# First pass in place: transposed rows written over x, sixteen tiles kept on chip, el and er twelve tiles behind, four statistics groups

## The chip, the cores and the metric

One core of one Trainium2 chip runs the kernel. The metric is device time in microseconds (us) of one execution. The engines are TensorE (PE, and PEld for its weight loads), VectorE (DVE), ScalarE (ACT), GpSimd (POOL) and SyncE (SP, which only issues transfers). SBUF is the on-chip memory of 128 partitions, PSUM the banks that TensorE writes.

## What is computed

Two layers of a graph network over N = 6250 nodes, E = 100000 edges sorted by dst, D = 512 features and 8 heads. In short form:

```python
h  = relu(layernorm(x))                                  # first pass
el = einsum((h @ W_src + b_src), attn_l)                 # per node and head
er = einsum((h @ W_dst + b_dst), attn_r)
v  = h @ W_val + b_val
e  = leaky_relu(el[src] + er[dst], 0.2)
a  = softmax of e over the edges of one dst
x  = x + segment_sum(v[src] * a, dst)                    # attention neighbour stage
h  = relu(layernorm(x))
x  = x + two GCN layers(h): relu(D^-1/2 (A + 2I) D^-1/2 h W + b), each
```

## The kernel before

The 6250 nodes are 49 tiles (TILES) of 128 rows. The order of the work is written by hand: every engine has its own program, and semaphores join them. What one engine waits for holds everything behind it in its program, its transfers included.

**First pass.** x is loaded in chunks of 8 tiles (XL) into `big`: three chunks from ScalarE's queue, three and the last tile from SP's, behind the weights. VectorE takes the statistics of each tile (`statistics`), and makes scale and bias for a group of tiles (`moments`), with a square root on ScalarE between (`deviations`). The groups are GROUPED = (0, 8, 24, 49). ScalarE normalises tile k into a buffer in `rows`; TensorE transposes it into a bank `tr`; ScalarE copies the bank to one of four buffers `ht_out` (HT = 4); TensorE multiplies that copy with 16 columns of folded weights into `sm` (this gives el and er, one tile behind the transposes); SP stores the copy to `ht_tab` in HBM. A buffer is free again when its store has landed and its product is done: `act.wait_ge(ht_kept[t % HT], t // HT * 16)` (L1340). Every fourth tile ScalarE copies el and er of four tiles (L1348) and TensorE turns them back (L1556). The folded weights come from GpSimd products (L1206, L1207) that wait for both pairs of weights, and from VectorE reductions (L492, L494).

**The row search.** VectorE compares node numbers with borders of the dst list (`find_rows`, L510), GpSimd then fetches rows of the list by indirect transfers (`seek_ring`, L1216), seven to a group, and VectorE counts in them (`count_in_rows`, L523). It ends in the in-degree of every node and its place in the edge list.

**V tiles.** v = h W_val is made tile by tile from the transposed rows. ScalarE reloads them from `ht_tab` into `ht_ring` (L1317), TensorE makes a tile with 4 matmuls of 512 columns (`value`, L1566), ScalarE copies it out (L1361) and stores it to `v_tab` (L1365). TensorE fills its waits with these tiles: V1 = 14 of them stand between the small products that prepare the tables (L1579 to L1607), ahead of the one-hot **picks** of el[src] (L1621, from 207 to 570 us); the other 35 stand among the edge softmax's waits. V_AT tells after how many tiles TensorE takes up each of the three carries of VectorE's scans (L1657, L1661); W_AT after how many it turns a half block of edge weights (L1650, eight of them, copied out alternately by VectorE at L834 and ScalarE at L1394); EXP_AT ahead of which tile ScalarE runs the two exponentials (L1385). VectorE clears `big` in two pieces at the end (L838, L841). Then GpSimd gathers rows of V, two gathers of 128 rows to a unit (L1280, 782 in all), once all V tiles are stored.

```python
V_AT = (V1 + 11, V1 + 19, V1 + 29)
EXP_AT = (V1 + 25, V1 + 25)
W_AT = (V1 + 32, V1 + 32, V1 + 33, V1 + 33, V1 + 34, V1 + 34, TILES, TILES)
```

Of the kernel before, what the change touches and what calls it, by code (L numbers as in the profile page):

```python
# [68 lines left out]
GROUPED = (0, 8, 24, TILES)  # L69
# [5 lines left out]
Q = 4  # L75
# [5 lines left out]
V1 = 14  # L81
V_AT = (V1 + 11, V1 + 19, V1 + 29)
EXP_AT = (V1 + 25, V1 + 25)
W_AT = (V1 + 32, V1 + 32, V1 + 33, V1 + 33, V1 + 34, V1 + 34, TILES, TILES)
HT = 4
ER_LOAD = 104
# [36 lines left out]
def build(nc, x, src, dst, W_src, b_src, W_dst, b_dst, W_val, b_val, attn_l, attn_r, W1, b1, W2, b2, out):  # L123
    ctx = ExitStack()
    with ctx:
# [140 lines left out]
        below = part(SEEK * (ROW // 2 + 1)).bitcast(BF16).rearrange("p (s n) -> p s n", s=SEEK)  # L266
# [23 lines left out]
        scanned = part.at  # L290
        ht_ring = part(HT * D).rearrange("p (s n) -> p s n", s=HT)
        ringed = part.at
# [11 lines left out]
        g_from = part(CUT.blocks ** 2 * P // 2).bitcast(BF16).rearrange("p (g n) -> p g n", n=CUT.blocks * P)  # L304

# [6 lines left out]
        def ht_out(slot):  # L312
            return rows[:, (4, 5, 0, 1)[slot], :]
# [4 lines left out]
        def first(t):  # L318
# [15 lines left out]
        pad_set, const_set, ident_set, edges_kept, fold_in, edges_in, dst_in = map(sem, (  # L334
            "pad_set", "const_set", "ident_set", "edges_kept", "fold_in", "edges_in", "dst_in"))
# [11 lines left out]
        wval_in, fold_loads = fold_in, 6  # L347
# [13 lines left out]
        ht_kept, low_before = low_in, [16 * len(range(n, TILES, HT)) for n in range(HT)]  # L361
# [41 lines left out]

        def all_kept(eng, pair, per=16):
            eng.wait_ge(pair[0], per * ((TILES + 1) // 2))
            eng.wait_ge(pair[1], per * (TILES // 2))
# [17 lines left out]

        prep, pe_steps = [0], [0]
# [3 lines left out]
        def _(dve):  # L429
# [38 lines left out]
            def moments(n, at):  # L468
# [9 lines left out]
                dve.scalar_tensor_tensor(ln[:, 1, at], ln[:, 3, at], 0.25, ln[:, 2, at], ALU.mult, ALU.add).then_inc(ln_set, 1)  # L478
                dve.wait_ge(std_set, n + 1)
# [6 lines left out]
            moments(0, slice(0, GROUPED[1]))  # L486
            statistics(range(1, 2))

            for s in range(2):
# [6 lines left out]
            dve.wait_ge(folded, 10)  # L496
            statistics(range(2, 3))
            dve.wait_ge(stat_set, GROUPED[2])
            moments(1, slice(GROUPED[1], GROUPED[2]))

# [51 lines left out]
            moments(2, slice(GROUPED[2], TILES))  # L552
# [17 lines left out]

            dve.wait_ge(h_set, TILES)
# [233 lines left out]
            dve.wait_ge(std_set, 4)  # L805
# [204 lines left out]
        def _(sp):  # L1010
# [4 lines left out]
            sp.dma_start(W_src_sb[:, :, :], W_src.rearrange("(k p) n -> p k n", p=P)).then_inc(fold_in, 16)  # L1015
            sp.dma_start(attn_sb[:, 0, :], on_all(attn_l.rearrange("h f -> (h f)"))).then_inc(fold_in, 16)
            sp.dma_start(bsd_sb[:, 0, :], on_all(b_src)).then_inc(fold_in, 16)
            sp.dma_start(W_dst_sb, W_dst.rearrange("(k p) n -> p k n", p=P)).then_inc(fold_in, 16)
            sp.dma_start(attn_sb[:, 1, :], on_all(attn_r.rearrange("h f -> (h f)"))).then_inc(fold_in, 16)
            sp.dma_start(bsd_sb[:, 1, :], on_all(b_dst)).then_inc(fold_in, 16)  # L1020
# [22 lines left out]
            for t in range(TILES):  # L1043
                sp.wait_ge(hT_set, t + 1)
                sp.dma_start(ht_tab[t, :, :], ht_out(t % HT)).then_inc(ht_kept[t % HT], 16)
                if t in (8, 11):
                    sp.wait_ge(edges_kept, 64)
                    load_firsts((8, 11).index(t))
                if t == 22:
                    sp.dma_start(src_flat[:, 0:J], src_rows.rearrange("g e -> (g e)").rearrange(  # L1050
                        "(p j) -> p j", j=J)).then_inc(edges_in, 16)
                if t == 26:
                    sp.dma_start(dst_i, dst_flat).then_inc(dst_in, 16)
                if t == 30:
                    sp.wait_ge(folded, 10)
                    sp.dma_start(wmat[:, :, 0:D], W_val.rearrange("(k p) n -> p k n", p=P)).then_inc(wval_in, 16)
                if t == 36:
# [8 lines left out]
            sp.wait_ge(h_set, TILES)  # L1066
            sp.wait_ge(dve_prep, marks["ends_of_units"])
# [6 lines left out]
            for n in range(HT):  # L1074
                sp.wait_ge(ht_kept[n], 16 * len(range(n, TILES, HT)))
# [105 lines left out]
        def _(pool):  # L1181
# [22 lines left out]
            pool.wait_ge(fold_in, 16 * fold_loads)  # L1204
            for s, w in enumerate((W_src_sb, W_dst_sb)):
                pool.tensor_tensor(bfold[:, s, :], bsd_sb[:, s, :], attn_sb[:, s, :], ALU.mult).then_inc(dve_setup, 1)  # L1206
                pool.tensor_tensor(fold[:, s, :, :], w[:, :, :], attn_sb[:, s, :].unsqueeze(1).to_broadcast([P, KC, D]),  # L1207
                                   ALU.mult).then_inc(dve_setup, 1)
            pool.wait_ge(edges_kept, 64)
            by_row = dst_rows.rearrange("g e -> (g e)").rearrange("(r e) -> r e", e=ROW)  # L1210
# [8 lines left out]
            pool.wait_ge(h_set, TILES)  # L1219
# [90 lines left out]
        def _(act):  # L1310
# [5 lines left out]
            def load_ht(t, slot):  # L1316
                act.dma_start(ht_ring[:, slot, :], ht_tab[ds(t, 1), :, :].rearrange("a p n -> p (a n)")).then_inc(ht_in[slot], 16)  # L1317

            def deviations(n, at):
                act.wait_ge(ln_set, 9 * n + 7)  # L1320
                act.activation(ln[:, 3, at], ln[:, 1, at], ACT.Sqrt, bias=epsc[:, 0:1]).then_inc(std_set, 1)
                act.wait_ge(ln_set, 9 * n + 9)
            deviations(0, slice(GROUPED[0], GROUPED[1]))
# [418 lines left out]
```

## Time and profile before

| | us |
|---|---|
| median of 3 runs (4145.99 to 4148.17) | 4147.86 |
| profiled execution, span | 4150.1 |
| start to first one-hot pick | 207.55 |
| last pick to first gather of V rows, from 570 to | 746.16 |
| busy in the span: PE / DVE / ACT / POOL | 3489.9 / 2288.9 / 1798.3 / 2607.4 |

The time reported for an execution and the span of the profiled one are of the same kind; the profile's span is 2.2 us above the median. The busy shares are those of stages with different limits, so the stretches up to 746 us have to be read one by one: in the windows what each engine did, in the waits who held whom, in the timeline when each step began, and in the chain of waits what ended last.

### The profile page before, as it was taken

What the parts mean: (1) busy time and instruction counts of PE and PEld (TensorE: products, weight loads), DVE (VectorE), ACT (ScalarE), POOL (GpSimd) and SP (SyncE); (2) the same over time, 40 slices, a digit from 0 to 9 for tenths busy, and PEclk for the clock granted to TensorE, in tenths of its full rate; (3) what the DMA queues carried; (4) which work ended last, traced back from release to release, by engine and by line L of the source; (5) the groups of instructions that cost most, each with busy time, mean ns of one, the idle gap of its engine ahead of it and who ended that gap; (6) DMA issues with size and microseconds to landing.
All of it is one profiled execution on the core that took longest, in us unless ns stands there. A gap on an engine that the chain in (4) does not pass through costs nothing.

```text
span 4150.1 us, 55488 instructions
## 1 busy us (share of the span) xinstructions
PE 3489.9 (84%) x15160; PEld 1694.2 (41%) x15160; DVE 2288.9 (55%) x3880; ACT 1798.3 (43%) x4172; POOL 2607.4 (63%) x2733
## 2 busy tenths in 40 slices
PE   5899988677888888898788888888997788888887
PEld 4499963222233333343333333333443333333332
DVE  6599887677777888885222333333552222333336
ACT  4356522444545555454333443444343333344442
POOL 3654411677777777654777777777106777777775
PEclk9999999899999999999999999999998999999999
DMA  7822325577777777665777777777216777777779
GB/s 285 244 67 61 90 76 208 172 210 210 210 210 211 210 210 211 190 206 190 210 210 210 210 210 210 211 210 210 79 66 211 211 210 210 210 210 210 210 209 351
DMA packets 318375, 804.24 MB, mean 194 GB/s; under 512 B 72905, under 2 KB 98139, under 8 KB 317129
## 3 DMA queue, kind: packets, MB, share of 16 engines
q0 software_dynamic: 199680, 630.72, 52.6%
q1 hardware_dynamic: 88925, 116.91, 8.5%
q10 hardware_dynamic: 29580, 54.49, 3.8%
q8 instruction: 67, 1.10, 0.1%
q14 instruction: 123, 1.01, 0.1%
HBM read 714.52 MB, written 88.21 MB: 193 GB/s over the span
## 4 chain that ended last, share of the span: by engine, by line
PE 34%; POOL 23%; issue 21%; DMA 12%; DVE 6%; SPq 1%; POOLq 1%; DVEq 1%; ACT 1%; ACTq 0%
POOL edge L1280 17%; PE mm L1529 8%; POOL rows_wmat L1280 5%; DMA edge<-h_tab,src_group 5%; DMA rows_wmat<-v_tab,src_group 4%; PE mm L1621 4%; PE sm L1693 4%; PE tr L1621 4%; PE mm L1693 4%; PE sm L1566 3%; PE tr L1693 2%; DVE edge L866 2%; PE tr L1524 1%; DMA ht_tab<-rows_wmat 1%; PE hist_ps L1693 1%
## 5 line engine op out<-in xcount | busy, mean ns | idle before, releaser
L1280 POOL DMA_INDIRECT edge<-h_tab,src_group x1564 | 1484.2, 949 | 708.5 <-issue 447.5
L1436 ACT ACTIVATE hots<-iota,drel 128x128 f32<-128x128 f32 x1760 | 538.0, 388 | 1174.5 <-PE tr L1693 606.9
L1280 POOL DMA_INDIRECT rows_wmat<-v_tab,src_group x782 | 739.4, 945 | 289.2 <-issue 272.4
L1693 PE MATMUL mm<-edge,hots 128*128 x880 | 465.9, 679 | 195.3 <-SPq L1098 189.7
L1693 PE MATMUL sm<-edge,hots 128*128 x880 | 442.6, 650 | 150.5 <-SPq L1098 148.1
L891 DVE TENSOR_TENSOR big<-big,mm 128x512 f32 x220 | 151.4, 688 | 686.6 <-PE tr L1693 668.8
L891 DVE TENSOR_TENSOR big<-big,sm 128x512 f32 x220 | 151.4, 688 | 602.6 <-PE misc L1693 588.6
L1693 PE MATMUL tr<-edge,hots 128*128 x880 | 395.6, 592 | 0.0
L1693 PEld LDWEIGHTS mm<-edge,hots 128*128 128x128 f32 x880 | 183.6, 217 | 470.1 <-issue 469.9
L1529 PE MATMUL mm<-rows_wmat 128*128 128x512 f32 x784 | 356.0, 598 | 0.0
L1693 PEld LDWEIGHTS sm<-edge,hots 128*128 128x128 f32 x880 | 175.8, 207 | 410.3 <-issue 410.0
L1673 PE MATMUL mm<-edge,hots 128*128 128x512 f32 x592 | 277.6, 608 | 65.0 <-ACT hots L1422 39.9
L1673 PE MATMUL sm<-edge,hots 128*128 128x512 f32 x584 | 275.5, 602 | 54.0 <-issue 27.6
L866 DVE TENSOR_TENSOR edge<-rows_wmat,tr 128x1024 f32<-128x1024 f32 x224 | 272.4, 1217 | 83.7 <-SPq L1098 83.6
L1422 ACT ACTIVATE hots<-eler_hots,ones 128x256 f32<-128x256 f32 x440 | 223.6, 508 | 203.4 <-PE sm L1673 71.0
L866 DVE TENSOR_TENSOR edge<-rows_wmat,misc 128x1024 f32<-128x1024 f32 x216 | 262.8, 1217 | 81.0 <-SPq L1098 80.9
L1417 ACT ACTIVATE eler_hots<-iota,drel 128x128 f32<-128x128 f32 x880 | 298.2, 386 | 0.0
L1239 POOL DMA_INDIRECT edge<-el_tab,src_flat x154 | 147.5, 958 | 180.0 <-DVE rows_wmat L690 157.6
L1439 ACT ACTIVATE hots<-hots,ones 128x1024 f32<-128x1024 f32 x220 | 252.6, 1148 | 7.1
L1693 PEld LDWEIGHTS tr<-edge,hots 128*128 128x128 f32 x880 | 167.4, 190 | 212.1 <-issue 212.1
L1693 PE MATMUL hist_ps<-edge,hots 128*128 x440 | 206.8, 592 | 0.0
L1693 PE MATMUL misc<-edge,hots 128*128 x440 | 206.8, 592 | 0.0
(252 smaller groups left out, 4574.0 us busy)
## 6 DMA issues: line engine op xcount, KB each, us to landing
h_tab<-rows_wmat SPq DMA_DIRECT2D x98, 256.0 KB, 2.0
edge<-h_tab,src_group POOLq DMA_INDIRECT x1564, 3.7
rows_wmat<-low_tab SPq DMA_DIRECT2D x157, 128.0 KB
ht_tab<-rows_wmat SPq DMA_DIRECT2D x49, 256.0 KB
big<-ht_tab ACTq DMA_DIRECT2D x49, 256.0 KB, 2.8
v_tab<-rows_wmat ACTq DMA_DIRECT2D x49, 256.0 KB
x_tab<-big SPq DMA_DIRECT2D x49, 256.0 KB, 2.1
rows_wmat<-v_tab,src_group POOLq DMA_INDIRECT x782, 3.7
```

Source lines behind the costliest of these rows:

```text
L866: dve.tensor_tensor(msgs[:, k % MSGS, :, :].rearrange("p c (h f) -> p c h f", f=F), got, weights.unsqueeze(3).to_broadcast([P, 2, H, F]), ...
L891: dve.tensor_tensor(big[:, ds(o, D)], big[:, ds(o, D)], agg_ps[bank][:, :], ALU.add).then_inc(a["acc_added"], 1)
L1239: pool.indirect_dma_start(el[:, at, :], None, el_tab, bass.IndirectOffsetOnAxis(ap=src_flat[:, at:at + 1], axis=0)).then_inc(el_in[n // AH ...
L1280: pool.indirect_dma_start(ring[:, 2 * u + c, :], None, tab, bass.IndirectOffsetOnAxis(ap=src_group[:, n:n + 1], axis=0)).then_inc(a["rows_ ...
L1417: act.activation(dist[:, n % 2, c, :], iota[:, :], ACT.Abs, bias=drel[:, n * 2 + c:n * 2 + c + 1], scale=-1.0).then_inc(a["dist_set"], 1)
L1422: act.activation(onehot[:, n % HOTS, :, :], dist[:, n % 2, :, :], ACT.Relu, bias=ones[:, 0:1], scale=-1.0).then_inc(a["onehot_set"], 1)
L1436: act.activation(group_hots[:, q % 2, e, :], iota[:, :], ACT.Abs, bias=drel[:, col:col + 1], scale=-1.0).then_inc(a["dist_set"], 1)
L1439: act.activation(group_hots[:, q % 2, :, :], group_hots[:, q % 2, :, :], ACT.Relu, bias=ones[:, 0:1], scale=-1.0).then_inc(a["onehot_set"], 1)
L1529: last = nc.tensor.matmul(bank, rows[:, slot, k * P:(k + 1) * P], rhs(k), start=(k == 0), stop=(k == KC - 1))
L1621: last = pe.matmul(sum_ps[bank][:, q * NA * H:(q + 1) * NA * H], src_hot[:, par, kt, q * P:(q + 1) * P], el_parts[:, part, kt, :, :], star ...
L1673: last = pe.matmul(gat_ps[w % GAT_SUMS][:, :], onehot[:, w % HOTS, n, :], msgs[:, w % MSGS, n, :], start=(n == 0), stop=(n == 1))
L1693: last = pe.matmul(agg_ps[bank][:, :], group_hots[:, q % 2, w % GROUP * 2 + n, :], edge[:, ds(slot[w % OFFS] + n * D, D)], start=(n == 0), ...
```

## The change

Transposed rows are no longer copied to four buffers but over x in `big`, each tile over its own (`first(t)`). The el/er products read them there, and run LAGGED = 12 tiles behind the transposes instead of one. Only the first 33 tiles (STORED) are stored to `ht_tab`, from `big`; the other sixteen stay where they are, and V1 = 16 V tiles are made from them ahead of the picks (V_ORDER puts them first). The other 33 are reloaded into four buffers of `rows` (`reloaded`), two ahead of the picks and two behind them. Statistics come in four groups, GROUPED = (0, 8, 16, 32, 49), and each group's scales (`scales`) stand apart from its `moments`, with folds and row searches between them. The folds of W_src no longer wait for W_dst. V_AT, EXP_AT, W_AT and the places of SP's index loads follow. `ht_ring` is gone from `big`, so the second clearing shrinks from 6144 to 4096 columns.

```diff
-GROUPED = (0, 8, 24, TILES)
+GROUPED = (0, 8, 16, 32, TILES)
-V1 = 14
-V_AT = (V1 + 11, V1 + 19, V1 + 29)
-EXP_AT = (V1 + 25, V1 + 25)
+STORED = 33
+V1 = TILES - STORED
+LAGGED = 12
+V_AT = (V1 + 11, V1 + 18, V1 + 28)
+EXP_AT = (V1 + 23, V1 + 23)
...
+V_ORDER = (*range(STORED, TILES), *range(STORED))
...
-        ht_ring = part(HT * D).rearrange("p (s n) -> p s n", s=HT)
-        ringed = part.at
+        scanned = ringed = part.at
...
-        def ht_out(slot):
-            return rows[:, (4, 5, 0, 1)[slot], :]
+        def reloaded(slot):
+            return rows[:, (6, 7, 2, 3)[slot], :]
...
+            dve.wait_ge(stat_set, GROUPED[2])
+            moments(1, at_group[1])
+            fold_side(0)
+            scales(1, at_group[1])
             turned()
-            for g in range(4):
-                find_rows(g)
-            statistics(range(GROUPED[2] // XL, TILES // XL))
+            find_rows(0)
+            fold_side(1)
+            statistics(range(2, 4))
+            dve.wait_ge(stat_set, GROUPED[3])
+            moments(2, at_group[2])
+            find_rows(1)
+            scales(2, at_group[2])
+            statistics(range(GROUPED[3] // XL, TILES // XL))
...
-            moments(2, slice(GROUPED[2], TILES))
+            moments(3, at_group[3])
+            find_rows(2)
+            scales(3, at_group[3])
+            find_rows(3)
+            dve.wait_ge(folded, 10)
...
-            for t in range(TILES):
+            for t in range(STORED):
                 sp.wait_ge(hT_set, t + 1)
-                sp.dma_start(ht_tab[t, :, :], ht_out(t % HT)).then_inc(ht_kept[t % HT], 16)
+                sp.dma_start(ht_tab[t, :, :], first(t)).then_inc(ht_kept[t % HT], 16)
...
-            for k in range(TILES + 6):
-                if k in GROUPED[1:3]:
-                    n = GROUPED.index(k)
-                    deviations(n, slice(GROUPED[n], GROUPED[n + 1]))
+            for k in range(TILES + LAGGED + 5):
+                if k + 1 in GROUPED[1:-1]:
+                    n = GROUPED.index(k + 1)
+                    deviations(n, at_group[n])
                 if k < TILES:
                     t = k
+                    if t in GROUPED:
+                        act.wait_ge(ln_set, 9 * (GROUPED.index(t) + 1))
...
-                    if t >= HT:
-                        act.wait_ge(eler_sum, t - (HT - 1))
-                        act.wait_ge(ht_kept[t % HT], t // HT * 16)
-                    act.activation(ht_out(t % HT), tr[t % 2][:, :], ACT.Copy).then_inc(hT_set, 1)
+                    act.activation(first(t), tr[t % 2][:, :], ACT.Copy).then_inc(hT_set, 1)
...
+            values(0, V1 - 1)
+            all_ht_kept(act)
+            act.wait_ge(eler_turned, -(-TILES // 4))
+            for n in range(2):
+                load_ht(n)
+            values(V1 - 1, V1)
...
-                if 1 <= k <= TILES:
-                    t = k - 1
+                if LAGGED <= k < TILES + LAGGED:
+                    t = k - LAGGED
```

How the order moves. VectorE, from the second chunk's statistics on (L466 before and L474 after are the statistics, L492/L494 and L504/L506 the folds, L510 and L517 the row search, L480 and L491 the first step of the scales). Before, after the loop of the second chunk:

```order
L492 TENSOR_REDUCE rows_wmat<-edge 128x8 x4
L494 TENSOR_REDUCE blr<-edge 128x8
L492 TENSOR_REDUCE rows_wmat<-edge 128x8 x4
L494 TENSOR_REDUCE blr<-edge 128x8
L463 UNCONDITIONAL_BRANCH
```

After, behind the same chunk:

```order
L486 SCALAR_TENSOR_TENSOR small<-small 128x8
L504 TENSOR_REDUCE rows_wmat<-edge 128x8 x4
L506 TENSOR_REDUCE blr<-edge 128x8
L491 RECIPROCAL small<-small 128x8
L493 SCALAR_TENSOR_TENSOR small<-small 128x8
L517 TENSOR_SCALAR hots,small<-hist_ps,small 128x255 x7
L520 CAST er_idx<-small 128x7
L504 TENSOR_REDUCE rows_wmat<-edge 128x8 x4
L506 TENSOR_REDUCE blr<-edge 128x8
L471 UNCONDITIONAL_BRANCH
```

The second group now has its moments right behind its chunk, then one fold, then its scales; the first row search and the second fold come ahead of the third chunk's loop.

TensorE at the end of the edge softmax, behind the third carry (L1566 and L1599 are V tiles, L1650 and L1683 the half blocks of weights). Before:

```order
L1566 MATMUL sm1<-rows_wmat,big 128x512 x4
L1650 MATMUL tr0<-ident,big 128x128 x4
L1650 MATMUL tr1<-ident,big 128x128 x4
L1650 MATMUL tr0<-ident,big 128x128 x4
L1650 MATMUL tr1<-ident,big 128x128 x4
L1566 MATMUL sm0<-rows_wmat,big 128x512 x4
L1650 MATMUL tr0<-ident,big 128x128 x4
L1650 MATMUL tr1<-ident,big 128x128 x4
L1650 MATMUL tr0<-ident,big 128x128 x4
L1650 MATMUL tr1<-ident,big 128x128 x4
```

After:

```order
L1599 MATMUL sm0<-rows_wmat 128x512 x4
L1683 MATMUL tr0<-ident,big 128x128 x4
L1683 MATMUL tr1<-ident,big 128x128 x4
L1683 MATMUL tr0<-ident,big 128x128 x4
L1683 MATMUL tr1<-ident,big 128x128 x4
L1683 MATMUL tr0<-ident,big 128x128 x4
L1683 MATMUL tr1<-ident,big 128x128 x4
L1683 MATMUL tr0<-ident,big 128x128 x4
L1683 MATMUL tr1<-ident,big 128x128 x4
```

The last V tile moved ahead of the last four half blocks; before, it stood between them.

## Rows read from the trace of the kernel before

**Rows 1.** Waits up to 210 us (total, times, longest), and two windows.

```profile
ACT rows_wmat L1341 <- DMA ht_tab<-rows_wmat: 19.6, 8, 6.0
...
core 0: us, PE busy (x) PEld busy (x) DVE busy (x) ACT busy (x) POOL busy (x), PEclk, DMA share, GB/s
120.00:130.00 10.00, 10.00 (x81) 7.10 (x78) 5.03 (x20) 8.15 (x13) 6.35 (x8) 1.00 0.82 264
140.00:150.00 10.00, 2.06 (x7) 1.18 (x8) 9.02 (x26) 0.27 (x1) 1.33 (x2) 0.67 0.81 170
```

**Rows 2.** Timeline of the first 64 us: start, duration, instruction, idle before.

```profile
11.29 4.85 DVE L466 BATCH_NORM_STATS2 big<-big  x8 [2.03 <-DMA big<-x]
...
17.89 1.52 ACT L1333 ACTIVATE rows_wmat<-big,small 128x512 f32<-128x512 f32 x2 [0.47 <-DVE small L482]
...
22.66 4.84 DVE L466 BATCH_NORM_STATS2 big<-big  x8 [4.81 <-DMA big<-x]
...
30.60 2.46 DVE L492 TENSOR_REDUCE rows_wmat<-edge 128x8 f32<-128x512 f32 x4 [3.10 <-POOL edge L1207]
...
42.27 18.73 SPq L1045 DMA_DIRECT2D ht_tab<-rows_wmat  x9
...
55.75 1.89 PE L1548 MATMUL sm<-rows_wmat 128*16 128x128 f32 x8
...
60.01 0.17 DVE L513 CAST er_idx<-small 128x7 int32<-128x7 f32 x1
...
63.17 0.32 DVE L513 CAST er_idx<-small 128x7 int32<-128x7 f32 x1
```

**Rows 3.** Timelines of TensorE, VectorE and ScalarE, 129 to 208 us.

```profile
129.41 0.66 PE L1524 MATMUL tr<-ident,rows_wmat 128*128 128x128 f32 x4
130.00 1.05 PE L1548 MATMUL sm<-rows_wmat 128*16 128x128 f32 x8
130.98 0.42 PE L1556 MATMUL mm<-ident,rows_wmat 16*128 16x16 f32 x4
131.32 0.66 PE L1524 MATMUL tr<-ident,rows_wmat 128*128 128x128 f32 x4
...
148.48 26.84 PE L1566 MATMUL sm<-rows_wmat,big 128*128 128x512 f32 x56 [7.92 <-DMA big<-ht_tab]
...
175.92 0.21 DVE L613 COPY small<-misc 128x49 f32<-128x49 f32 x1 [12.97 <-PE misc L1580]
...
204.69 0.60 ACT L1361 ACTIVATE rows_wmat<-sm 128x512 f32<-128x512 f32 x1 [2.84 <-PE sm L1566]
...
207.55 5.63 PE L1621 MATMUL mm<-big,edge 128*128 128x104 bf16 x84 [2.90 <-ACT edge L1378]
```

**Rows 4.** Chain of waits, 545 to 800 us: start, duration, what.

```profile
620.84 29.59 PE sm L1566 x64
...
672.84 0.60 ACT rows_wmat L1361
...
680.75 12.07 DVE big L810 x15
...
720.42 8.87 DVE big L838
...
732.03 4.43 PE sm L1566 x8
...
738.87 3.45 PE sm L1566 x8
...
746.16 0.95 POOL rows_wmat L1280
```

**Rows 5.** Timeline of VectorE in the same stretch.

```profile
650.75 0.41 DVE L713 COPY big<-misc 8x256 f32<-8x256 f32 x1 [3.22 <-PE misc L1657]
...
746.27 5.18 DVE L841 MEMSET big<- 128x6144 f32 x1 [1.90 <-issue]
753.97 2.35 DVE L866 TENSOR_TENSOR edge<-rows_wmat,tr 128x1024 f32<-128x1024 f32 x2 [2.52 <-SPq L1098]
```

**Rows 6.** The page's groups: the gathers of V rows.

```profile
L1280 POOL DMA_INDIRECT rows_wmat<-v_tab,src_group x782 | 739.4, 945 | 289.2 <-issue 272.4
```

More of the change, by code:

```diff
@@ L360, in build @@
         low_in = [sem(f"low_in{b}") for b in range(4)]
[L361 removed]
+        ht_kept, low_before = low_in, [16 * len(range(n, STORED, HT)) for n in range(HT)]
         gcn_rows_in = [sem(f"gcn_rows_in{u}") for u in range(RING[1] // 2)]
@@ L402, in all_landed, with all_ht_kept @@
                     eng.wait_ge(pair[b], 16 * n)
+        def all_ht_kept(eng):
+            for n in range(HT):
+                eng.wait_ge(ht_kept[n], low_before[n])
         def all_kept(eng, pair, per=16):
@@ L485, in _, with fold_side @@
             dve.wait_ge(stat_set, GROUPED[1])
-            moments(0, slice(0, GROUPED[1]))
+            moments(0, at_group[0])
+            scales(0, at_group[0])
             statistics(range(1, 2))
-            for s in range(2):
+            def fold_side(s):
                 dve.wait_ge(dve_setup, 2 * s + 2)
@@ L1380, in _ @@
             pipelined(act, PCOLS // Q, 4, 0, far)
+            act.wait_ge(el_picked, PCOLS // Q)
+            for n in range(2, HT):
+                load_ht(n)
             def exponentials(half):
@@ L1530, in product @@
                 last.then_inc(done, 1)
-            for k in range(TILES + 8):
+            for k in range(TILES + LAGGED + 7):
                 if k < TILES:
@@ L1548, in _ @@
                         last = pe.matmul(sm[q % 2][0:2 * H, n * P:(n + 1) * P], wmat[:, kc, D:D + 2 * H],
-                                         ht_out(t % HT)[:, kc * P:(kc + 1) * P], start=(kc == 0), stop=(kc == KC - 1))
+                                         first(t)[:, kc * P:(kc + 1) * P], start=(kc == 0), stop=(kc == KC - 1))
                     last.then_inc(eler_sum, 1)
-                if k >= 8 and k % 4 == 0:
-                    q = k // 4 - 2
-                    pe.wait_ge(elerT_set, q + 1)
-                    for t in range(4 * q, min(4 * q + 4, TILES)):
-                        at = t % (D // (2 * H)) * 2 * H
-                        last = pe.transpose(mm[t // (D // (2 * H))][:, at:at + 2 * H], elerT[:, q % 2, t % 4 * P:(t % 4 + 1) * P],
-                                            ident[0:2 * H, 0:2 * H])
-                    last.then_inc(eler_turned, 1)
@@ L1560, in value @@
-            def value(s):
-                t, par = s.k, s.j % 2
-                pe.wait_ge(ht_in[s.j], (t - s.j) * 4 + 32)
-                if s.past(2):
-                    pe.wait_ge(v_set, t - 1)
+                if k >= LAGGED + 7 and (k - LAGGED - 7) % 4 == 0:
+                    q = (k - LAGGED - 7) // 4
+                    if q * 4 < TILES:
+                        pe.wait_ge(elerT_set, q + 1)
+                        for t in range(4 * q, min(4 * q + 4, TILES)):
+                            at = t % (D // (2 * H)) * 2 * H
+                            last = pe.transpose(mm[t // (D // (2 * H))][:, at:at + 2 * H], elerT[:, q % 2, t % 4 * P:(t % 4 + 1) * P],
+                                                ident[0:2 * H, 0:2 * H])
+                        last.then_inc(eler_turned, 1)
@@ L1565, in value @@
+            pe.wait_ge(elerT_set, -(-TILES // 4))
+            def value(c):
+                t = V_ORDER[c]
+                if c < V1:
+                    pe.wait_ge(hT_set, t + 1)
+                    source = first(t)
+                else:
+                    pe.wait_ge(ht_in[t % HT], t // HT * 16 + 32)
+                    source = reloaded(t % HT)
+                if c >= 2:
+                    pe.wait_ge(v_set, c - 1)
                 for k in range(KC):
-                    last = pe.matmul(sm[par][:, :], ht_ring[:, s.j, k * P:(k + 1) * P], wmat[:, k, 0:D],
+                    last = pe.matmul(sm[c % 2][:, :], source[:, k * P:(k + 1) * P], wmat[:, k, 0:D],
```

106 lines of the change are left out of this document (52 added, 54 removed).

## The prediction

> **What bounds the kernel now.** The page was read first: the picks, the three aggregations and the dense layers between them fill most of the 4150.1 us, and the change touches none of their code. So only two stretches count: from the start to the first one-hot pick (207.55 us, last row of [rows 3]), and from the end of the picks to the first gather of V rows (746.16 us, [rows 4]). Whatever starts those two long stages earlier moves the end by as much, since nothing in them hangs on absolute time.
>
> In the first stretch I read the waits and then the timeline. ScalarE stood 19.6 us waiting for a store of transposed rows to leave its buffer [rows 1]: the first store is issued only at 42.27 us, behind the loads of x in SP's queue [rows 2]. Where nothing is late TensorE sets the pace: one tile is a transpose and an el/er product, 129.41 to 130.98, 1.57 us, and every fourth tile adds 0.34 for turning el and er back (130.98 to 131.32) [rows 3]. Then TensorE waits 7.92 us for a reload and begins the V tiles at 148.48 [rows 3]. VectorE's row search is hidden there: at 175.92 it had waited 12.97 us for TensorE [rows 3]. So from 148.48 to 207.55 TensorE is the path: fourteen V tiles of 3.44 us each (0.60 busy and 2.84 of waiting in the ScalarE row at 204.69), small products between them, and 2.9 us of ScalarE at the end [rows 3].
>
> In the second stretch the chain of waits alternates between VectorE's scans and V tiles on TensorE: 29.59 us for eight tiles, then tiles again up to the ScalarE copy at 672.84, which stands in ScalarE's order ahead of the exponentials; then sums, a clearing of 8.87 us, one V tile at 732.03 and the last at 738.87 [rows 4].
>
> **Part 1: the first pass.** Stores and reloads no longer hold ScalarE, since it copies over x. What is late next is the statistics. Tile 8 needs chunk 1, whose statistics end at 22.66 + 4.84 = 27.5. A group's small steps take 17.89 - 16.14 = 1.75 us in all with ScalarE's root, 1.3 of it on VectorE [rows 2]. With the src fold reduction (2.46 and a short one after it, 3.1) placed between them, group 2's scales stand at 27.5 + 1.3 + 3.1 = 32 us. Tiles 16 to 31 need more: one row search (63.17 - 60.01 = 3.2), the dst fold (3.1), two chunks of statistics (2 x 4.84 = 9.7), a second row search (3.2) and small steps (1.3): 32 + 20.5 = 52.5 [rows 2]. x itself isn't late, since SP has issued all its x loads before 42.27 and the chunk needed last there is the fourth of six. ScalarE is blocked at tile 15 meanwhile (its root stands ahead of that tile), and TensorE behind it; the first transpose of tile 16 can start at 53.3.
>
> From there TensorE has 33 transposes (0.59 each, 129.41 to 130.00), 45 el/er products (0.98, 130.00 to 130.98) and 13 turns back (0.34) [rows 3]: 19.5 + 44.1 + 4.4 = 68.0 us. The twelve-tile lag costs nothing in work; it only keeps the products from waiting for a copy or for the folds (ready at 38, wanted by tile 0's product at about 38). A restart after a pause costs up to 2.8 us (26.84 us for seven V tiles that are worth 24.1) [rows 3]; the pause here is shorter and broken by tile 15, so I take 2, between 0.5 and 2.8. ScalarE needs about 1.4 us a tile (two normalisations in 1.52 [rows 2], a copy of 0.60) against 1.65, so it follows. The fourth group waits for ScalarE at tile 31, not for VectorE, which has those chunks done by about 64. The V tiles then start at 53.3 + 68.0 + 2 = 123.3, which is 25.2 us earlier.
>
> **Part 2: V tiles before the picks.** Sixteen instead of fourteen: + 2 x 3.44 = 6.9. TensorE comes to them without the 7.92 us wait, so the low clock of that restart goes: - 2.8. The picks start 25.2 - 6.9 + 2.8 = **21.1 us earlier**, at 186.5.
>
> The clock has to be weighed here. In 140 to 150 us, around the wait for the reload, the granted clock was 0.67, and in 120 to 130, with dense work, 1.00 [rows 1]; the el/er product took 1.89 us at 55.75 and 0.98 at 130.00 [rows 2, 3]. The Trainium skill, TensorE: Matmul & The Clock Gate, section "A second HAM failure mode: psum-queue depth-cycling", warns that short waits between groups of matmuls, as when buffers are cycled, can make the clock fall again and again. By that rule the 68.0 us above would be longer; by the rows of 120 to 130, where the same groups cycle through the same two banks, they are not. I keep the rows.
>
> Cover: with V tiles from 123.3, TensorE asks for the row search's result at about 147.4. The search starts at 32 instead of 57 and its seeks alternate with it; I estimate its end, the scans behind it included, at 146 to 150, so the 12.97 us of slack shrinks to almost nothing. It is taken at nothing, and up to +3 kept for the range. SP's order is moved too: 33 stores instead of 49, with the index loads earlier, all ahead of need. The wait for all stores stands in front of work on four engines, but by the pace above the last of the 33 is issued some 40 us before the first of these asks, so it costs nothing.
>
> **Part 3: after the picks.** Thirty-three V tiles instead of thirty-five, and the two missing ones are missing on the path. (a) Between the first and the second carry, seven tiles instead of eight: VectorE waited 3.22 us there [rows 5], TensorE is 3.44 earlier, so - 2.8, after which VectorE is the later. (b) Ahead of the exponentials five tiles instead of six: the copy at 672.84 comes at 672.84 - 2.8 - 3.4 = 666.6; the 7.9 us from it to the sums (680.75) stay, so the sums begin at 674.5, **6.25 earlier**. (c) Up to the V tile at 732.03 all shifts by 6.25, to 725.8; it takes 4.43 and is now the last, where before 738.87 followed. From a last tile's end (742.32) to the first gather were 3.84 us [rows 4]; now 730.2 + 3.84 = 734.05. That is **12.1 us earlier**. (d) What could be late next is VectorE: four remaining weight turns (about 6 us) and the clearing, cut from 5.18 to 5.18 x 4096/6144 = 3.45, end near 741; the first rows come 753.97 - 746.16 = 7.8 after the gather begins, at 741.9 [rows 5]. Just in time. The stage behind is paced by GpSimd's 782 gathers, 739.4 us busy and 272.4 us of issue [rows 6], so an early gather counts in full.
>
> **Sum.** 21.1 + 12.1 = 33.2 us. The profiled span is 4150.1 us, 2.2 above the median of 4147.9 (0.05%, inside what executions differ by); 4150.1 - 33.2 = 4116.9, and on the median 4147.9 - 33.2 = **4114.7 us**. From 0.2%, 8.3 us, a measurement can tell a difference.
>
> **Rivals.** (A) The row search becomes the bound between first pass and picks. For: the slack is nearly gone. If it is not earlier at all, TensorE passes it at 163 instead of 147.4, and parts 1 and 2 give 21.1 - 15.6 = 5.5: total 18, 4130 us. With a half of that, 4122. Against: its first seeks are issued 25 us earlier. Chance 0.12. (B) Part 3 gives only the last tile and not the exponentials, because VectorE or the store of the sums is later than counted: 4 to 6 instead of 12, so 4121. Chance 0.09. (C) No change: the first pass isn't held by stores but by statistics that take as long again (chunks landing late, POOL's folds slower beside VectorE), so that tile 16 starts at 75 rather than 53, and part 3 fails as in B: 4140 to 4148. Chance 0.04. (D) Slower: TensorE stays at its low level (1.2 GHz) through the first pass. The place is tile 16 to the last el/er product; the products take 1.89 instead of 0.98 us [rows 2, 3], and if all scales so, 68.0 becomes 131, + 63. With all of it low the kernel ends at 4178; it is slower from 53% of that stretch on. Against: 1.00 in 120 to 130 [rows 1]. The page TensorE: Matmul & The Clock Gate of the Trainium skill, by the section named above, would give part of this. Chance 0.02.
>
> The forecast itself (4108 to 4120) has 0.73. The range, 4105 to 4128, takes in A's half, B, and below the forecast 9 us for a first pass without the restart and a second stretch that saves more. Faster by over 0.2%: 0.94; within: 0.04; slower: 0.02.
>
> **What would show it.** In the changed profile: no wait of ScalarE for a store; tile 16's normalisation near 52.5; V tiles from 123; first pick near 186.5; the exponentials right behind a copy at about 645.5 (666.6 - 21.1); the first V gather near 713; then the same pace. Wrong would be: VectorE or GpSimd as the last releaser of TensorE between 123 and 186, a granted clock near 0.5 for tens of us before 120, or a first gather that waits for anything but the last V tile's store.

## The result

| | us | ratio to before |
|---|---|---|
| before, median of 3 (4145.99 to 4148.17) | 4147.9 | |
| changed kernel, median of 4 (4116.75 to 4125.68) | 4119.4 | 0.9937, 95% interval 0.9924 to 0.995 |
| changed kernel again, on another chip (before there 4148.3) | 4119.3 | 0.9930, 0.9913 to 0.9947 |

The change makes the kernel 28.5 us faster; 33.2 were predicted. A fourth execution of before, at 17647.01 us, was in a slow state and is left out. The ratios with their intervals are estimates over the executions and not the quotients of the two medians (4119.4 / 4147.9 would be 0.9931). The time of an execution is its span + 1.8 us (4125.68 and 4123.9 for the profiled one), not, as the part ahead of the prediction has it, the span itself.

**Profile after.** The timeline of the first pass, from the point where the third group's scales are ready (columns: start, duration, engine, line, operation, and in brackets the idle time before it and who ended it; line numbers are the changed kernel's):

```profile
53.66 1.11 PE L1550 MATMUL tr<-ident,rows_wmat 128*128 128x128 f32 x4 [5.89 <-ACT rows_wmat L1356]
56.13 0.81 ACT L1356 ACTIVATE rows_wmat<-big,small 128x512 f32<-128x512 f32 x1 [2.04 <-DVE small L493]
56.99 1.12 PE L1550 MATMUL tr<-ident,rows_wmat 128*128 128x128 f32 x4 [0.40 <-ACT rows_wmat L1356]
...
124.29 24.30 PE L1599 MATMUL sm<-rows_wmat,big 128*128 128x512 f32 x56
...
153.10 0.63 PE L1620 MATMUL misc<-ident,edge 128*128 128x128 f32 x4 [0.38 <-DVE hist L637]
...
187.96 6.06 PE L1654 MATMUL mm<-big,edge 128*128 128x104 bf16 x96 [2.88 <-ACT edge L1401]
```

These answer [rows 3]. Tile 16 is normalised at 56.13, its transpose is at 56.99; the V tiles start at 124.29, and the seven of them take 24.30 us where 26.84 stood, since no wait for a reload stands ahead of them: the granted clock is 1.00 from 124 to 150 us, where before had 0.67 from 140 to 150 [rows 1]. The 0.38 us at 153.10 is all that TensorE waits for the row search: its slack is gone, but it costs nothing yet. No wait of ScalarE for a store of transposed rows is left. Its longest waits up to 150 us are now for VectorE's statistics (19.6 us in three) and for V tiles on TensorE (15.3 us in five).

Behind the picks, timeline of ScalarE, VectorE, TensorE and GpSimd [rows 4, 5]:

```profile
645.89 0.60 ACT L1375 ACTIVATE rows_wmat<-sm 128x512 f32<-128x512 f32 x1 [2.84 <-PE sm L1599]
653.79 1.59 DVE L831 SCALAR_TENSOR_TENSOR big<-big,edge 128x782 f32<-128x782 f32 x1 [5.08 <-ACT edge L1411]
693.35 8.85 DVE L859 MEMSET big<- 128x10555 f32 x1 [8.61 <-issue]
704.75 4.50 PE L1599 MATMUL sm<-rows_wmat 128*128 128x512 f32 x8
712.76 0.95 POOL L1302 DMA_INDIRECT rows_wmat<-v_tab,src_group  x1 [44.79 <-DMA v_tab<-rows_wmat]
721.12 2.35 DVE L887 TENSOR_TENSOR edge<-rows_wmat,tr 128x1024 f32<-128x1024 f32 x2 [1.53 <-SPq L1118]
```

The copy ahead of the exponentials is at 645.89, the last V tile at 704.75 and the first gather at 712.76, released by the last V store. The first message (VectorE's product of gathered rows with their weights) comes at 721.12, 1.53 us behind the end of the second clearing. The row names SP's counting of landed rows, but e4 below has the same pause of 1.52 us with rows gathered long before, so the clearing and what follows it set this time.

In the groups of the page, the gathers of V rows that [rows 6] showed for before:

```profile
L1302 POOL DMA_INDIRECT rows_wmat<-v_tab,src_group x782 | 741.6, 948 | 282.9 <-issue 218.9
```

So the first gather came 33.4 us earlier than in the first profile of before, the predicted amount nearly to the digit (by luck, as the second pair of profiles shows), and yet the span is only 26.2 us shorter. The experiments had to say where 7 us went.

### The profile page after: what moved, and what is told of

The parts are those of the page before. It is cut to its first block, busy times and chain, and to the rows that moved or that the text cites. A ratio compares the mean times of both kernels' runs of the same rounds, so it can differ in the third digit from the quotient of the medians.

```text
span 4123.9 us, 55381 instructions
## 1 busy us (share of the span) xinstructions
PE 3493.6 (85%) x15160; PEld 1695.3 (41%) x15160; DVE 2288.8 (56%) x3889; ACT 1798.8 (44%) x4173; POOL 2618.4 (63%) x2733
## 3 DMA queue, kind: packets, MB, share of 16 engines
q0 software_dynamic: 199680, 630.72, 53.3%
## 4 chain that ended last, share of the span: by engine, by line
PE 29%; POOL 26%; issue 23%; DMA 11%; DVE 8%; POOLq 1%; DVEq 1%; ACT 1%; ACTq 0%; SPq 0%
POOL edge L1302 20%; PE mm L1555 8%; POOL rows_wmat L1302 6%; DMA rows_wmat<-v_tab,src_group 5%; PE mm L1654 4%; PE tr L1654 4%; DMA edge<-h_tab,src_group 4%; PE sm L1726 3%; PE mm L1726 3%; DVE edge L887 2%; PE tr L1726 2%; PE tr L1550 1%; PE sm L1599 1%; DVE big L897 1%; PE hist_ps L1726 1%
## 5 line engine op out<-in xcount | busy, mean ns | idle before, releaser
L1726 PE MATMUL sm<-edge,hots 128*128 x880 | 476.6, 692 | 153.4 <-SPq L1118 152.6
L1726 PE MATMUL mm<-edge,hots 128*128 x880 | 441.7, 649 | 187.9 <-SPq L1118 184.4
L1726 PEld LDWEIGHTS sm<-edge,hots 128*128 128x128 f32 x880 | 189.0, 222 | 431.3 <-issue 431.3
L1726 PEld LDWEIGHTS mm<-edge,hots 128*128 128x128 f32 x880 | 174.0, 206 | 450.2 <-issue 450.2
```

Of the source, the lines that this page charges most:

```text
L1726: last = pe.matmul(agg_ps[bank][:, :], group_hots[:, q % 2, w % GROUP * 2 + n, :], edge[:, ds(slot[w % OFFS] + n * D, D)], start=(n == 0), ...
```

## The experiments

All times below are medians; the chips differ, so each ratio is to before on the same chip. e1 to e4 ran on one chip, e5 to e8 on another, e9 to e11 on a third (before: 4149.35, 4148.3 and 4153.3). The changed kernel was timed on the second of them only; e1 to e4 and e9 to e11 are set against it by way of these ratios.

### Both kernels a second time (e5, e6)

> The kernel before, unchanged, profiled a second time. From the first gather of V rows to the end its first profile took 3403.9 us, the same as three experiments (3403.1 to 3403.8), while the changed kernel's profile took 3411.1. Theory (executions differ in the gathers, and the first profile of before was itself some 3 us long ahead of the gathers): the tail again within 1 us of 3403.5 and the first gather between 741 and 746, span 4145 to 4150. Rival (before always reaches its gathers at 746.2): 746.2 within 0.5.

> The changed kernel, unchanged, profiled a second time and timed beside the others. Theory (the 7 us by which its first profile's tail was longer belong to that execution): tail 3403 to 3404, first gather at 712 to 714, span 4116 to 4118, time 4118 to 4120. Rival (the change itself slows the gathers, through what it leaves in memory or queues): tail again near 3411.

Timeline rows of before's second profile, and then of the changed kernel's:

```profile
143.75 26.81 PE L1566 MATMUL sm<-rows_wmat,big 128*128 128x512 f32 x56 [8.47 <-DMA big<-ht_tab]
202.53 6.18 PE L1621 MATMUL mm<-big,edge 128*128 128x104 bf16 x96 [2.90 <-ACT edge L1378]
741.11 0.95 POOL L1280 DMA_INDIRECT rows_wmat<-v_tab,src_group  x1 [51.74 <-issue]
```

```profile
125.10 24.30 PE L1599 MATMUL sm<-rows_wmat,big 128*128 128x512 f32 x56
188.19 4.59 PE L1654 MATMUL mm<-big,edge 128*128 128x104 bf16 x96 [2.88 <-ACT edge L1401]
714.77 0.95 POOL L1302 DMA_INDIRECT rows_wmat<-v_tab,src_group  x1 [44.98 <-DMA v_tab<-rows_wmat]
```

| us | before, 1st | before, 2nd | forecast | after, 1st | after, 2nd |
|---|---|---|---|---|---|
| V tiles start | 148.48 | 143.75 | 123.3 | 124.29 | 125.10 |
| first pick | 207.55 | 202.53 | 186.5 | 187.96 | 188.19 |
| sums begin | 680.75 | 675.23 | 653.4 | 653.79 | 655.64 |
| first V gather | 746.16 | 741.11 | 713 | 712.76 | 714.77 |
| from there to the end | 3403.9 | 3404.2 | | 3411.1 | 3403.3 |
| span | 4150.1 | 4145.3 | 4116.9 | 4123.9 | 4118.1 |

Both theories hold in the main; e6's first gather came 0.8 us and its span 0.1 us later than its theory allowed. The 7 us in the tail are not the changed kernel's as such, since its second profile does not have them. They lie in all three stages of gathers: 963.7 us from the thirteenth to the last gather of V rows (961.4 in e6), then 978.7 (976.5) and 984.6 (981.2) for the two stages behind. Nor do they belong to one execution alone: e11's profile has 963.6, 978.6 and 984.6. The other eleven profiles, both of before among them, lie at 961.2 to 961.5, 976.2 to 976.5 and 979.4 to 982.9. What makes the gathers slower in two profiles of thirteen is open.

And the first profile of before was long ahead of the gathers. Its waits for stores of transposed rows, first and second profile:

```profile
ACT rows_wmat L1341 <- DMA ht_tab<-rows_wmat: 15.9, 8, 6.7
```

That is 15.9 us against the 19.6 of [rows 1], 3.7 us less, where the V tiles start 4.7 us earlier. TensorE's granted clock differed too, 0.83 against 0.91 from 100 to 120 us, so the 3.7 us are the likely main part and not a proof. The second pair of profiles gives 27.2 us between the spans; the medians give 28.5.

### One wait for the stores put back (e1)

```diff
+                    if HT <= t < STORED + HT:
+                        act.wait_ge(ht_kept[t % HT], t // HT * 16)
                     act.activation(first(t), tr[t % 2][:, :], ACT.Copy).then_inc(hT_set, 1)
```

> The changed kernel with one wait put back: ScalarE copies tile t over x only when the store of tile t - 4 has landed, as with the four buffers of before. Theory (part 1: the wait for stores held the first pass): SP issues its first store at 42.1 us and the fifth is stuck in the queue to 58.8, so the copy of tile 8 waits until about 60.5. From there TensorE has about 39 transposes, 49 products and 13 turns back, 23 + 48 + 4.4 = 75 us; V tiles start near 137 instead of 124.3, the picks 12 us later than 187.96, and the time is near 4131. Rival (statistics hold the first pass, the stores are hidden behind them): tile 16 still starts at 56 to 60, V tiles within 4 us of 124.3, time 4118 to 4123.

Measured: 4142.2, ratio 0.998 (0.997 to 0.999); V tiles at 144.21, first gather at 736.81. The waits of ScalarE and of VectorE up to 150 us (total, times, longest):

```profile
ACT big L1363 <- DMA ht_tab<-big: 27.6, 3, 25.2
```

```profile
DVE small L491 <- ACT small L1343: 29.4, 3, 17.8
```

The theory holds and was too small: 19 to 20 us at the V tiles instead of 13. The expectation counted ScalarE's copies only. But the square roots of the next groups stand behind a blocked copy in ScalarE's program, so VectorE waited 17.8 us for one of them, with the second fold and the row search behind that wait. With this one wait back, all the rest, part 3 included, is worth only 0.2% over before. By the ratios (0.998 against 0.9930 and 0.9937) 18 to 21 of the 26 to 29 us hang on that wait being gone, in the order of the changed kernel. What writing in place alone would give in the order of before was not run.

### The lag of el/er (e2), and the row search behind it (e7, e10)

```diff
-LAGGED = 12
+LAGGED = 6
```

> The changed kernel with el/er products 6 instead of 12 tiles behind the transposes. TensorE stood idle for 5.9 us ahead of tile 16; with the shorter lag 6 more products (0.98 us each) run ahead of it. Theory (the row search has become as late as TensorE): V tiles start 5 to 6 us earlier, near 118.5, but the small product behind the seventh V tile now waits 4 to 6 us for VectorE's place counts (144.0), the first pick stays within 1 us of 187.96 and the time at 4119. Rival (the search still has slack): the first pick is 5 us earlier, 183, and the time 4114.

Measured: 4124.9, ratio 0.9941 (0.9924 to 0.9958). Timelines of TensorE and VectorE:

```profile
120.54 24.30 PE L1599 MATMUL sm<-rows_wmat,big 128*128 128x512 f32 x56
...
146.06 0.42 PE L1612 MATMUL misc<-small,shift 128*128 128x49 f32 x2 [1.22 <-DVE small L615]
...
155.01 0.63 PE L1620 MATMUL misc<-ident,edge 128*128 128x128 f32 x4 [4.54 <-DVE hist L637]
...
155.59 5.29 PE L1599 MATMUL sm<-rows_wmat,big 128*128 128x512 f32 x8
...
191.54 4.59 PE L1654 MATMUL mm<-big,edge 128*128 128x104 bf16 x96 [2.88 <-ACT edge L1401]
```

The V tiles start 3.8 to 4.6 us earlier, and TensorE then waits 5.8 us for VectorE: the search has become the bound. The first pick is not the same as expected but 3.5 us later. About 1.8 us are a slip of the search itself (its place counts at 145.8 instead of 144.0), and 1.7 us the V tiles behind the wait, which take 5.29 us where the changed kernel has 3.60: the granted clock was 0.83 from 150 to 160 us, and 1.00 in the changed kernel. Why the search was so late showed in the changed kernel's VectorE and GpSimd:

```profile
67.27 0.18 DVE L486 SCALAR_TENSOR_TENSOR small<-small 128x17 f32<-128x17 f32 x1
...
80.51 0.27 DVE L491 RECIPROCAL small<-small 128x17 f32<-128x17 f32 x1 [10.03 <-ACT small L1343]
...
84.06 0.62 DVE L530 TENSOR_SCALAR_CACHE_REDUCE hots<-edge,small 128x391 bf16<-128x391 int32 x1
```

```profile
88.68 0.95 POOL L1237 DMA_INDIRECT edge<-dst_rows,er_idx  x1 [24.36 <-DVE hots L530]
```

VectorE waits 10.03 us for the last group's root, which ScalarE computes only ahead of tile 31; the first counts stand behind it, and GpSimd, whose ring holds two groups of seeks, waits 24.36 us for them. With lag 6 the wait grew to 11.57. e7 and e10 move the counts:

```diff
             find_rows(2)
+            find_rows(3)
+            for g in range(2):
+                count_in_rows(g)
             scales(3, at_group[3])
-            find_rows(3)
```

> Lag 6 as before, and on VectorE the search steps moved: rows 3 and the counts of the first two groups stand ahead of the last group's scales, behind which they had waited 10 to 12 us for ScalarE's root (L491). Theory (the row search was the bound with lag 6, and it was late by that wait): seeks of group 2 start near 78 instead of 88.7, the place counts are ready before TensorE asks, V tiles start near 120.5 as with lag 6, TensorE does not wait for VectorE up to the picks, and the first pick comes at 184 instead of 191.5, so 4 us ahead of the changed kernel: 4115. Rival (the search is bound by its fetches' time, not by that wait): the first pick at 188 or later.

> The changed kernel (lag 12) with only the search steps on VectorE moved ahead of the last group's scales. Theory (at lag 12 TensorE and the search come out together, so neither alone gives anything): place counts ready near 136 instead of 144.0, no wait of TensorE for VectorE behind the V tiles, the first pick only 0.4 to 0.8 us earlier, 187 to 188.2, time 4117 to 4120. Rival (the search is the later of the two): the first pick 3 us or more earlier, time 4115.

e7: 4117.5, ratio 0.9924 (0.9907 to 0.994). e10: ratio 0.9937 (0.992 to 0.9953), its four times between 4114.8 and 4130.0. Rows of e7, then of e10:

```profile
79.31 0.95 POOL L1236 DMA_INDIRECT edge<-dst_rows,er_idx  x1 [14.93 <-DVE hots L530]
...
121.24 24.30 PE L1598 MATMUL sm<-rows_wmat,big 128*128 128x512 f32 x56
...
135.63 0.21 DVE L614 SCALAR_TENSOR_TENSOR small<-small 128x49 f32<-128x49 f32 x1
...
184.49 6.03 PE L1653 MATMUL mm<-big,edge 128*128 128x104 bf16 x96 [2.88 <-ACT edge L1400]
```

```profile
124.28 24.30 PE L1598 MATMUL sm<-rows_wmat,big 128*128 128x512 f32 x56
...
187.48 6.18 PE L1653 MATMUL mm<-big,edge 128*128 128x104 bf16 x96 [2.88 <-ACT edge L1400]
```

Both as the theories said: with lag 12 the earlier search gives 0.5 to 0.7 us (187.48 against 187.96 and 188.19), and only with lag 6, where the search was the bound, it gives 7 (first pick at 184.49 instead of 191.54). But 3.4 us of that are lost behind the sums: from the sums to the first gather e7 takes 714.93 - 652.40 = 62.5 us and e2 62.6, the changed kernel 59.0 and 59.1. In e7 ScalarE's longest wait for a store of V between 590 and 720 us was 7.5 us. Why lag 6 lengthens this stretch is open. By their times e7 and e10 are not told apart from the changed kernel, so these readings rest on the profiles.

### The border between the second and third group of statistics (e9)

```diff
-GROUPED = (0, 8, 16, 32, TILES)
+GROUPED = (0, 8, 24, 32, TILES)
-            statistics(range(1, 2))
+            statistics(range(1, 3))
```

> The changed kernel with its second statistics group 16 tiles long, as before (GROUPED = 0, 8, 24, 32, 49; the third chunk's statistics move ahead of it). Theory (the fold for el/er and TensorE's amount of work set the first pass, not the number of groups): tile 8 starts at 38 instead of 33 and the fold comes 5 us later, near 47, but TensorE has no pause at tile 16; V tiles start at 122.5 to 125.5 (124.3 to 125.1 in the two profiles of the changed kernel), time 4117 to 4121. Rival (the finer groups are what brings the first pass forward): V tiles 4 us or more later, 129, time 4124.

Measured: 4127.7, ratio 0.994 (0.9923 to 0.9957), V tiles at 124.97, first el/er product at 50.78 instead of 42.90. For the V tiles it is as the theory said: a first fold 8 us later costs nothing, since TensorE has no pause at tile 16 afterwards. The row search does pay:

```profile
155.09 0.63 PE L1620 MATMUL misc<-ident,edge 128*128 128x128 f32 x4 [1.70 <-DVE hist L637]
...
190.19 6.19 PE L1654 MATMUL mm<-big,edge 128*128 128x104 bf16 x96 [2.88 <-ACT edge L1401]
```

TensorE waits 1.70 us for it instead of 0.38, and the first pick is 2.0 to 2.2 us later. So the border at tile 16 brings the V tiles nothing and the picks about 2 us. There are four groups in both kernels; what the number of groups is worth was not tried. The profile of e9 ends 42.8 us behind its last gather, the others 33.9 to 38.0, so its span says little.

### GpSimd's product and VectorE's small steps (e8)

```diff
                 pool.wait_ge(fold_in[s], 16 * fold_loads)
+                if s:
+                    pool.wait_ge(ln_set, 16)
```

> The changed kernel with one added wait: GpSimd starts the products of the second fold only behind the small steps of group 1 on VectorE. In the changed kernel a VectorE addition of 128x8 took 2.80 us at 29.15 instead of 0.17, and ended as GpSimd's product of 4.52 us, begun at 27.40, did. Theory (the two engines' two-input operations exclude each other): that addition takes 0.2 us, and tile 16, the V tiles and the first pick come 1.8 to 2.6 us earlier (V tiles at 121.7 to 122.5), time 4117. Rival (the long addition has another cause): it stays at 2.8 us, or the stall comes back at another operation, and the first pick stays at 188.

Changed kernel, then e8, VectorE and GpSimd:

```profile
29.15 2.80 DVE L478 TENSOR_TENSOR small<-big 128x8 f32<-128x8 f32 x1
...
27.40 4.52 POOL L1227 TENSOR_TENSOR edge<-edge 128x2048 f32<-128x2048 f32 x1
```

```profile
29.04 0.17 DVE L478 TENSOR_TENSOR small<-big 128x8 f32<-128x8 f32 x1
...
33.04 2.80 DVE L493 SCALAR_TENSOR_TENSOR small<-small 128x8 f32<-128x8 f32 x1
...
31.31 4.50 POOL L1229 TENSOR_TENSOR edge<-edge 128x2048 f32<-128x2048 f32 x1
```

The cause is borne out and the gain is not: the addition takes 0.17 us, but the next VectorE operation with two inputs that falls into the product, L493, is held until the product ends (31.31 + 4.50 = 35.8). The first pick is at 188.64, the ratio 0.9925 (0.9908 to 0.9942), not told apart from the changed kernel's. The reductions of the first fold (one input) took the usual 2.46 and 0.67 us beside the product. This agrees with the Trainium skill, SBUF — State Buffer, section "SBUF: two separate sides": a VectorE operation with two SBUF inputs and a GpSimd operation that reads SBUF take turns on one pair of ports, for a whole instruction.

### The order behind the picks (e3, e4)

```diff
-V_AT = (V1 + 11, V1 + 18, V1 + 28)
-EXP_AT = (V1 + 23, V1 + 23)
+V_AT = (V1 + 11, V1 + 19, V1 + 29)
+EXP_AT = (V1 + 25, V1 + 25)
```

> The changed kernel with the order of before between the carries: eight V tiles between carry 1 and carry 2, six from there to the exponentials (V_AT + 19 and + 29, EXP_AT + 25). Theory (steps a and b of part 3: 2.8 + 3.44 us hang on these two tiles): the copy ahead of the exponentials at 652.1 instead of 645.9, the sums 6.2 us later, the first gather of V rows at 719 instead of 712.8, time near 4125.5. Rival (the sums are held by something else, the store of the sums or VectorE): first gather within 2 us of 712.8 and time 4119 to 4121.

Measured: 4125.0, ratio 0.9939 (0.9922 to 0.9955). Against the changed kernel's two ratios that is 1 to 4 us more, inside the intervals, so the verdict rests on the profile. Its first pick was at 189.32; from there the sums begin 472.4 us later (661.67), in the changed kernel 465.8 and 467.5. That is 4.9 to 6.5 us later, where 6.2 were expected. One stall of TensorE in this stretch, told of at the end, differs from profile to profile; without it e3 has 459.3 us, and the ten profiles with the changed kernel's order 451.6 to 454.2. That is 6.4 us above their mean of 453.0: the exponentials and the sums do hang on these two tiles.

```profile
661.67 1.59 DVE L831 SCALAR_TENSOR_TENSOR big<-big,edge 128x782 f32<-128x782 f32 x1 [8.51 <-ACT edge L1411]
```

e4 goes further the same way:

```diff
-W_AT = (V1 + 31, V1 + 31, V1 + 32, V1 + 32, TILES, TILES, TILES, TILES)
+W_AT = (V1 + 32, V1 + 32, TILES, TILES, TILES, TILES, TILES, TILES)
```

> The changed kernel with both last V tiles ahead of the first turn of weights (W_AT + 32 twice, then all 33). VectorE waited 8.6 us ahead of its clearing for the store of the sums, so a V tile ahead of the first turn costs nothing there. Theory (the last V tile sets the first gather and, by the ring of 12 gathers, the stage): last V tile near 682, first gather near 690 instead of 712.8, all 12 slots filled before VectorE's first message, which comes 4 to 7 us earlier since TensorE has no V tile between the turns behind the clearing; the thirteenth gather, 727.8 in the changed kernel, comes at 716 to 719 and the time falls by 9 to 12 us to 4107 to 4110. Rival (the stage is set by VectorE's first message alone, which does not move): thirteenth gather at 722.5, time 4114. Second rival (gathers beside the clearing and the weights slow those down): 4119 or more.

Measured: 4113.5, ratio 0.9917 (0.9901 to 0.9934). First, twelfth and thirteenth gather, and the first message:

```profile
693.83 0.95 POOL L1302 DMA_INDIRECT rows_wmat<-v_tab,src_group  x1 [27.10 <-DMA v_tab<-rows_wmat]
707.56 0.94 POOL L1302 DMA_INDIRECT rows_wmat<-v_tab,src_group  x1 [0.30 <-issue]
720.95 0.94 POOL L1302 DMA_INDIRECT rows_wmat<-v_tab,src_group  x1 [12.45 <-DVE edge L887]
```

```profile
694.39 8.85 DVE L859 MEMSET big<- 128x10555 f32 x1 [9.72 <-issue]
...
713.93 3.47 DVE L862 MEMSET big<- 128x4096 f32 x1 [1.75 <-issue]
718.93 3.48 DVE L887 TENSOR_TENSOR edge<-rows_wmat,tr 128x1024 f32<-128x1024 f32 x3 [1.52 <-issue]
```

The gathers start 19 us earlier and fill the ring of twelve; then GpSimd waits 12.45 us for the first message. What counts is the thirteenth gather, 720.95 instead of 727.82 and 729.79: 6.9 to 8.8 us earlier, and by the ratios the time falls by 0.13 to 0.2%, 5 to 8 us. The expected 9 to 12 assumed an earlier first message; it moved by only 2.2 us. The clearing ahead of it, which waits for the store of the sums, began at 694.39, 1.0 us later than in the changed kernel (693.35), although the sums had begun 1.2 us earlier.

### All of it together (e11)

> All that the runs point to: both last V tiles ahead of the first turn of weights, the search's counts ahead of the last group's scales, the second fold ahead of the first row search, the second row search behind group 3's scales, lag 9. Theory (the terms add: the fold ready at 39 instead of 42, tile 16 at 53 instead of 56, no pause of TensorE): V tiles start at 117 to 119, the first pick at 180.5 to 183, 5 to 7 us earlier, and 6 us more from the last tile as measured: 4106 to 4109. Rival (the search or the stores behind the picks give it back, as the first 3 us of lag 6 were given back between the sums and the first gather): 4112 to 4114, no better than the early last tile alone.

Measured: 4117.0, ratio 0.9906 (0.9889 to 0.9922). Timelines of TensorE and GpSimd:

```profile
53.69 1.12 PE L1549 MATMUL tr<-ident,rows_wmat 128*128 128x128 f32 x4 [4.75 <-ACT rows_wmat L1355]
...
121.73 24.30 PE L1598 MATMUL sm<-rows_wmat,big 128*128 128x512 f32 x56
...
184.93 6.18 PE L1653 MATMUL mm<-big,edge 128*128 128x104 bf16 x96 [2.88 <-ACT edge L1400]
```

```profile
719.98 0.94 POOL L1301 DMA_INDIRECT rows_wmat<-v_tab,src_group  x1 [11.93 <-DVE edge L886]
```

The first pick is 3 us earlier and not 5 to 7, since TensorE still pauses 4.75 us ahead of tile 15; and at the thirteenth gather only 1 us of it is left against e4 (720.95). Up to there this profile lies with the rival. The forecast times do not carry over to this chip, where before took 4153.3 (0.9906 of 4148 would be 4109); the profile's end is not to be compared, since it is one of the two with slower gathers. By their ratios e4 and e11 both come out ahead of the changed kernel, but the intervals of e4 and of the changed kernel overlap, and so do those of e4 and e11. e11 has the best ratio seen; its upper end, 0.9922, lies ahead of both ratios of the changed kernel, but its interval still overlaps the one of e6 (0.9913 to 0.9947), measured on another chip.

## Why the prediction was right, and what was off

**Direction and mechanism: right.** The waits for the stores held the first pass (e1, 19 to 20 us at the V tiles), and the two tiles fewer ahead of the sums shorten the second stretch by about their own time (e3). That the first gather came 33.4 us earlier in the first pair of profiles, where 33.2 were forecast, is luck: 1.5 us less than forecast up to the picks and 1.7 us more behind them, against a profile of before that was itself 5 us late. The second pair has 26.3 us (741.11 - 714.77).

**Part 1.** The positions hold: tile 16 at 56.13 instead of 52.5, V tiles at 124.29 and 125.10 instead of 123.3. The 3.6 us of the first have two causes: the statistics of chunk 1 began at 24.26 instead of 22.66, and GpSimd's product held VectorE's next step for 2.6 us; the steps behind took 0.6 us less than counted. That the second is such a hold is e8's finding. The 68.0 us of TensorE's work, with 2 us for a restart, were 124.29 - 56.99 = 67.3 in all, so 2.7 of the 3.7 us at the first transpose (56.99 against 53.3) came back. Rival D, a TensorE that stays slow, did not occur, nor a clock that falls again and again: it was 0.98 from 57 to 80 us and 1.00 from there to 124 (0.93 and 1.00 in the second profile).

**Part 2.** First pick at 188.0 and 188.2 instead of 186.5: 1.0 us came from part 1, and the slack of the row search was taken at nothing and was 0.38 us of waiting. Rival A was one step away: with TensorE 4 us earlier (e2) it waited 5.8 us for the search.

**Part 3.** Between first pick and first gather lie 538.61 and 538.58 us in the two profiles of before and 524.80 and 526.58 in those of the changed kernel: 12.0 to 13.8 less, 12.1 predicted. (a) and (b) together are confirmed by e3; why (a) takes 2.8 us of the 3.22 that VectorE waited is not said there, and only 0.4 us hang on it. (c), the last tile, was not tried alone. (d) "Just in time" was right: the first message came at 721.12, and the thirteenth gather, which waits for it, went out at the usual pace (0.31 us of idle time before it).

**The term that was mis-sized** is the start of parts 1 and 2, "the picks start 21.1 us earlier": it was 19.6 in the first pair of profiles and 14.3 in the second. The end of that difference was forecast within 1.7 us; its beginning, 207.55, was one execution's, 5 us later than the next one's, in large part by store waits that vary (19.6 and 15.9 us). The medians side with the second pair: 28.5 us less the 12.0 to 13.8 of part 3 leave 14.7 to 16.5. The prediction put the profiled span 2.2 us above the median. Times lie 1.8 us above spans, so it was 4.0, and a difference formed against it gives that much too much: 4151.9 - 33.2 would have been 4118.7. The median before did not contain these 4 us, and the 33.2 took them off all the same; they are most of the 4.7 us between 4114.7 and 4119.4.

## What to carry to other kernels

When a change removes a wait that varies, its gain has to be counted against a typical execution and not against the one in the profile: read the same wait in a second profile first. A sum that meets one profile to the digit is no proof until a second profile gives it too. A blocked step holds back all that stands behind it in its engine's program: the returned store wait cost 20 us and not 13, because square roots stood behind it, and a search's counts came 10 us late behind a root that nobody else needed yet. Work that fills a ring early is worth only what it moves the first step that needs a freed slot.

## What the runs showed of the hardware

One of the 33 store issues in SP's queue of the changed kernel took 13.5 us (durations in ns, least, median, most), a few us behind the last loads of x. The second profile has it too, with 13.6 us, while the longest in before's two profiles took 6.3 and 5.4 us. With buffers that wait for stores, ScalarE inherits such a stall (e1).

```profile
L1066 SPq DMA_DIRECT2D ht_tab<-big x33: 423/750/13476, 42.1 to 90.7; - x33
```

The picks end with a stall of TensorE. Near its end a round of 96 matmuls takes 4.43 us, but the last full round took 11.7 to 15.6 us in every one of the thirteen profiles (11.7 and 13.9 in before, 12.7 and 15.6 in the changed kernel), with idle times that nothing recorded explains. Before's first profile, then the changed kernel's:

```profile
550.21 4.59 PE L1621 MATMUL mm<-big,edge 128*128 128x104 bf16 x96
...
564.26 2.32 PE L1621 MATMUL tr<-big,edge 128*128 128x104 bf16 x25 [3.97 <-issue]
```

```profile
543.48 3.97 PE L1654 MATMUL tr<-big,edge 128*128 128x104 bf16 x56 [6.61 <-issue]
```

In the ten profiles with the changed kernel's order from the first pick to the sums, this stretch took 463.6 (e10) to 468.7 us (e8), a spread larger than several of the effects tried here; without this round it is 2.6 us.
